# A transformer decoder layer on one core: the order in which each engine takes its tasks is replaced by another

## The reference

```python
x = x + attn(layernorm(x), Wq, Wk, Wv, Wo)            # 16 heads of 16, causal, alibi bias
x = x + xattn(layernorm(x), ctx, ctx, Wq, Wk, Wv, Wo) # 16 heads of 16, 120 keys
x = x + tanh(layernorm(x) @ weight @ aux_weight1 @ aux_weight2 + bias)
```

## Time and profile before

| | us |
|---|---|
| median of 3 runs | 2784.67 |
| lowest and highest of them | 2781.45, 2797.6 |
| profiled execution, time | 2791.88 |
| profiled execution, span from first to last instruction | 2790.1 |
| PE busy in the span | 2495.2 |
| DVE busy | 1714.9 |
| ACT busy | 1403.3 |
| POOL busy | 714.5 |

### The profile page before, as it was taken

How to read it: one execution, slowest core, us unless ns; L and a number is a source line. 1 busy time by engine, 2 the same in 40 slices (tenths; PEclk the granted TensorE clock), 3 DMA queues, 4 the chain that set the end, 5 groups by cost and what they waited for, 6 DMA issues and landing times.

```text
span 2790.1 us, 70718 instructions
## 1 busy us (share of the span) xinstructions
PE 2495.2 (89%) x23737; PEld 2048.2 (73%) x23864; DVE 1714.9 (61%) x3714; ACT 1403.3 (50%) x3067; POOL 714.5 (26%) x1359
## 2 busy tenths in 40 slices
...
GB/s 74 63 89 90 88 88 96 84 90 93 82 85 96 91 83 96 84 87 96 90 83 93 92 87 87 96 89 85 96 88 81 93 95 85 92 87 87 90 76 21
DMA packets 162889, 240.65 MB, mean 86 GB/s; under 512 B 21790, under 2 KB 86030, under 8 KB 159766
## 3 DMA queue, kind: packets, MB, share of 16 engines
...
...
## 4 chain that ended last, share of the span: by engine, by line
PE 57%; DMA 24%; DVE 6%; SPq 4%; issue 4%; ACT 4%; ACTq 1%; POOL 0%; DVEq 0%; POOLq 0%
DMA q_stack<-q_nat 12%; PE ps_misc L474 10%; DMA ctx_in<-in_ctx 9%; PE ps_misc L488 9%; PE ps_max L540 4%; SPq L394 4%; PE ps_score L585 3%; PE ps_score L572 3%; PE ps_max L553 3%; PE ps_attend L600 3%; PE ps_max L530 3%; PE ps_score L574 3%; PE ps_score L576 3%; PE ps_misc L630 2%; PE ps_max L536 2%
## 5 line engine op out<-in xcount | busy, mean ns | idle before, releaser
L901 DVE TENSOR_REDUCE neg_max_s<-ps_max 128x2 f32<-128x512 f32 (+1 forms) x768 | 483.1, 682 | 111.3 <-PE ps_max L530 73.0
L750 ACT ACTIVATE probs<-ps_score 128x384 f32<-128x384 f32 x1024 | 470.0, 492 | 141.3 <-PE ps_score L576 135.4
L757 ACT ACTIVATE xprobs<-ps_score 120x512 f32<-120x512 f32 x512 | 295.5, 599 | 244.4 <-PE ps_score L585 237.1
L1018 POOL TENSOR_SCALAR ve_LN<-mv_LN 128x2 f32<-128x2 f32 x192 | 36.8, 191 | 1342.7 <-DVE mv_LN L923 1342.7
L574 PE MATMUL ps_score<-q_stack,k_stack 97*128 97x256 f32 x1024 | 378.1, 369 | 0.0
L909 DVE TENSOR_REDUCE neg_max_x<-ps_max 128x4 f32<-128x480 f32 x512 | 314.2, 651 | 70.3 <-PE ps_max L553 70.3
L572 PE MATMUL ps_score<-mask_k,ident_b 128*128 128x256 bf16 x1024 | 290.9, 284 | 22.6 <-DMA q_stack<-neg_max_t_s 15.0
L576 PE MATMUL ps_score<-q_stack,k_stack 97*128 97x256 f32 x1024 | 291.1, 284 | 0.0
L1044 POOL TENSOR_TENSOR res<-res,chain_n 128x512 f32<-128x512 f32 x64 | 82.4, 1288 | 605.2 <-ACT chain_n L795 605.2
L585 PE MATMUL ps_score<-xq_stack,xk_stack 97*120 97x256 f32 x1024 | 227.2, 314 | 3.5 <-DMA xq_stack<-neg_max_t_x 2.8
L574 PEld LDWEIGHTS ps_score<-q_stack,k_stack 97*128 97x128 f32 x1024 | 206.6, 202 | 1.5
...
## 6 DMA issues: line engine op xcount, KB each, us to landing
k_stack<-k_nat SPq DMA_DIRECT2D x192, 256.0 KB, 6.9
q_stack<-q_nat SPq DMA_DIRECT2D x192, 256.0 KB, 7.2
xq_stack<-q_nat SPq DMA_DIRECT2D x192, 256.0 KB, 6.0
...
x_in<-in_x SPq DMA_DIRECT2D x64, 256.0 KB, 3.2
...
out_y<-res SPq DMA_DIRECT2D x64, 256.0 KB, 2.2
...
```

Source lines behind the costliest of these rows:

```text
L750: act.activation(probs[:, h % 8, :], bank_of("SCORE", i, b, h)[:, P:4 * P], ACT.Exp)\
L757: act.activation(xprobs[0:C, at:at + 2, :], blocks(bank_of("XSCORE", i, b, u))[0:C], ACT.Exp).then_inc(sem("xprobs_ready"), 1)
L901: dve.tensor_reduce(o, ins, AX.X, ALU.max, negate=True).then_inc(sem("max_taken"), 1)
```

## The change

All five tables are replaced. No instruction is added or taken away, no duration or size is changed; only the order on each engine, and with it the bank that each task gets, and the last step is one earlier (`END_STEP`), since the new tables need one step fewer to drain. Two lines of the tables and the constant, as the diff has them (each table is replaced as a whole, and its rows are better read in the order below):

```diff
 ORDER = {
     "SP": (
-        ("STORE", -3, 0), ("XMAX_STACK", -2, 0), ("LOAD_X", 1, 0), ("XK_STACK", -1, 0),
...
+        ("LOAD_X", 1, 0), ("XK_STACK", -1, 0), ("MAX_STACK", 0, 0), ("XQ_STACK", -1, 0),
+        ("LOAD_CTX", 0, 0), ("K_STACK", 1, 0), ("Q_STACK", 1, 0), ("STORE", -2, 0),
+        ("XMAX_STACK", -1, 0), ("XK_SAVE", 0, 0),
...
-FIRST_STEP, LOOP_FROM, LOOP_TO, END_STEP = -2, 6, 62, NSEQ + 3
+FIRST_STEP, LOOP_FROM, LOOP_TO, END_STEP = -2, 6, 62, NSEQ + 2
```

More of the change, by code:

```diff
@@ L68 @@
[L68 to L79, removed]
@@ L82 @@
+        ("LN2_T", 0, 0), ("XATTEND", -1, 1), ("MAX_T", 1, 0), ("XSCORE", -1, 6), ("XSCORE", -1, 7),
+        ("XQ", 0, 0), ("XATTEND", -1, 2), ("XATTEND", -1, 3), ("SCORE", 1, 0), ("SCORE", 1, 1),
+        ("XHEADS_OUT", -1, 0), ("XHEADS_OUT", -1, 1), ("SCORE", 1, 2), ("SCORE", 1, 3),
+        ("LN1_T", 2, 0), ("SCORE", 1, 4), ("SCORE", 1, 5), ("XOUT_T", -1, 0), ("ATTEND", 1, 0),
+        ("K", 2, 0), ("SCORE", 1, 6), ("SCORE", 1, 7),
     ),
     "ACT": (
-        ("SCORE", -1, 11), ("ATTEND", -1, 1), ("SCORE", -1, 12), ("SCORE", -1, 13),
@@ L85 @@
-        ("LN3_T", -3, 0), ("SCORE", -1, 14), ("SCORE", -1, 15), ("FFN", -3, 0), ("ATTEND", -1, 3),
-        ("V", 0, 0), ("XMAX_T", -2, 0), ("OUT_T", -1, 0), ("XSCORE", -2, 0), ("XSCORE", -2, 1),
-        ("XV", -1, 0), ("XSCORE", -2, 2), ("XSCORE", -2, 3), ("XSCORE", -2, 4), ("XSCORE", -2, 5),
-        ("XATTEND", -2, 1), ("XSCORE", -2, 6), ("XSCORE", -2, 7), ("LN2_T", -1, 0), ("MAX_T", 0, 0),
-        ("XATTEND", -2, 3), ("XQ", -1, 0), ("SCORE", 0, 0), ("SCORE", 0, 1), ("SCORE", 0, 2),
-        ("SCORE", 0, 3), ("LN1_T", 1, 0), ("SCORE", 0, 4), ("XOUT_T", -2, 0), ("K", 1, 0),
@@ L93 @@
+        ("LN3_T", -2, 0), ("SCORE", 0, 13), ("SCORE", 0, 14), ("CTX_T", 0, 0), ("SCORE", 0, 15),
+        ("FFN", -2, 0), ("ATTEND", 0, 3), ("XV", 0, 0), ("XMAX_T", -1, 0), ("OUT_T", 0, 0),
+        ("XK", 0, 0), ("XSCORE", -1, 0), ("XSCORE", -1, 1), ("V", 1, 0), ("XSCORE", -1, 2),
+        ("XSCORE", -1, 3), ("XSCORE", -1, 4), ("XSCORE", -1, 5), ("LN2_T", 0, 0), ("MAX_T", 1, 0),
+        ("XATTEND", -1, 1), ("XSCORE", -1, 6), ("XSCORE", -1, 7),
     ),
     "DVE": (
-        ("XMAX", -2, 2), ("XMAX", -2, 3), ("LN3_T", -3, 0), ("FFN", -3, 0), ("XMAX", -2, 4),
```

39 lines of the change are left out of this document (23 added, 16 removed).

## The result

The changed kernel takes 2816.3 us (median of 5 runs, 2798.73 to 2824.74) against 2790.8 of the kernel before on the same chip (5 runs). The ratio is 1.0088, with a 95% interval of 1.0054 to 1.0123: within 1%, as forecast, and on the slow side of it. Its profiled execution took 2798.73 us, the fastest of its five.

The account below looks back on a forecast made before the run. PE, 89% busy, was taken as the bound, with k and q transfers in turn setting when MAX starts. Cycle 81.0 plus 1.8 for the clock, 82.8 against 82.7, adds 3 us: 2795 profiled, 2788 median; range 2725 to 2856.

Parts of the forecast that it names:

- the sum at full clock: Four PE stretches added per step: 40.8 us even (with context work), 40.2 odd, a cycle of 81.0 us.
- MAX to OUT_PROJ: PE, first MAX to first OUT_PROJ matmul: 4.1 us even, 3.6 odd, the odd with 1.1 us standing for OUT_T.
- SCORE 0 to K: PE, first SCORE matmul to K's last: 6.45 us in both steps, bounds 6.3 and 6.8.
- The context wait: PE's 2.9 us wait for the context load in the even step: covered by work moved ahead, gone.
- K to MAX: PE, K's last matmul to first MAX: bound by k and q transfers in turn, 18.0 us even, 17.9 odd.
- OUT_PROJ to SCORE 0: PE, first OUT_PROJ to first SCORE matmul: grows by 1.1 us to 12.25 in both steps, bounds 0.2 and 1.5.
- DVE alone makes XQ late: Between OUT_PROJ and XQ: DVE's eight maxima instead of six delay LN2_T, so XQ starts at 1165.25 instead of 1164.99.
- the score stretch takes V for nothing: Faster rival, OUT_PROJ to SCORE 0: V fits into gaps, stretch grows 0.2 instead of 1.1 us; 2735 us, chance 0.27.
- XK_SAVE and XK_STACK: XK's save moved behind XMAX_STACK, its stack load ahead of MAX_STACK: cost nothing, cover 1.3 us.
- I leave the cost at 1.8: Slow PE clock behind waits: costs 1.8 us per cycle as before, bounds 0 and 5.0, making the cycle 82.8.
- The sign that was named: PE's granted clock over 1000 to 2500 us: 0.96 to 0.98; leaving that would show the forecast wrong.
- the clock falls behind both waits in every cycle: Slower rival, both waits before MAX: clock costs 4 us per cycle instead of 1.8; 2856 us, chance 0.27.

Follow-up runs that it names:

- experiment 1: The changed kernel with 246 skipped waits (123 instructions) ahead of PE's loop, moving its code; 2766.94 us, 0.9917 of the kernel before.
- Experiment 7: The changed kernel with the third of K's three transfers cut from 16 rows to one, so scores lack one product; 2630.49 us, one run.
- 8: The changed kernel with V alone put back ahead of XMAX 7 on PE and XV on ACT; 2744.69 us, 0.9841 of the kernel before.
- experiment 9: The changed kernel with V alone back in its old place and 123 instructions of skipped waits ahead of the loop; 2718.28 us, 0.9747 of before.
- experiment 10: The changed kernel with 123 skipped instructions and DVE's maxima 4 and 5 back ahead of OUT_PROJ's residual; 2770.08 us, 0.9928 of before.
- 11: The changed kernel with 123 skipped instructions and both V and DVE's maxima 4 and 5 back in their old places; 2709.82 us, 0.9718 of before.
- experiment 2: The kernel before with 266 skipped waits (133 instructions) ahead of PE's loop, moving its code; 2785.97 us, 0.9992 of the kernel before.

## Why the prediction was right or wrong

**The total** was 2788 and is 2816.3, within the range, and "within 1%" came true, with a gain and a loss behind it that nearly cancel. Without the stops the changed kernel is at 2767 (experiment 1), so the forecast was 21 us too high for what it reasoned about; the stops, about which it said nothing, add 49. That the sum of the two still lies in the range is luck. Of the 0.9 us by which the forecast cycle of 82.8 is above that of experiment 1 (81.94), the clock has 0.4 and the sum at full clock 0.4 to 0.5: three of its terms, MAX to OUT_PROJ in both steps and SCORE 0 to K, were each some 0.13 too high.

**The context wait** is gone, as forecast: no row of L507 for ctx_in is left.

**K to MAX** was called the sentence on which it all rests, 17.9 us in both steps. It is 18.2 in the even step and 18.1 in the odd one, with waits of 2.0 and 2.7 where 2.2 and 2.7 were given; 157.5 us in 64 waits where some 150 in 62 were. Experiment 7 shows the cause and 8 shows the other side, that 1.5 us of work put in there cost nothing.

**MAX to OUT_PROJ**: 3.96 for 4.1 in the even step. In the odd step a wait for DVE's chain_t comes as said, 0.7 us long behind the slow clock and 0.58 at full clock (experiment 9), where 1.1 was worked out. At full clock the stretch is 3.7 from the first weight load on (experiment 9), which by the cut of the forecast is 3.5 for 3.6.

**OUT_PROJ to SCORE 0** came to 12.2 as forecast. The steps inside it hold in part. The 1.1 us for XATTEND 2 and 3 behind XQ are there, measured at 0.8. The start of XQ, forecast 0.26 later, is: 9.64 us behind OUT_PROJ (1153.33 to 1162.97) instead of 9.34. The DVE row shows the eight maxima back to back, with a release of LN2_T at their end:

```profile
1155.06 0.69 DVE L955 TENSOR_TENSOR res<-ps_misc,x_in 128x512 f32<-128x512 f32 x1 [1.18 <-PE ps_misc L487]
...
1157.22 4.88 DVE L900 TENSOR_REDUCE neg_max_s<-ps_max 128x2 f32<-128x512 f32 x8 [0.28 <-issue]
1162.13 0.69 DVE L874 TENSOR_TENSOR chain_t<-ps_misc,chain_t 128x512 fp32r<-128x512 f32 x1
```

But that DVE alone makes XQ late is wrong. The way from OUT_PROJ to XQ, even / odd, is 9.3 / 9.3 us before and 9.6 / 9.6 after; it is 10.1 / 9.6 with DVE's order put back (experiment 10), 9.4 / 9.6 with V put back (9) and 9.4 / 9.3 with both (11). In the odd step either of the two is enough to make XQ late, and in the even step V is what does it. And the rival "the score stretch takes V for nothing" had half of the truth: V is nearly free there (0.3 us per cycle in experiment 9), but the stretch grows by 1 us all the same, for another reason, so its 2735 did not come.

**SCORE 0 to K**: 6.32 for 6.45. **XK_SAVE and XK_STACK** cost nothing, as forecast.

**The clock is the term that was mis-sized.** "I leave the cost at 1.8": it is 1.4 us in the cycle above, and 1.4 in the mean cycle of experiment 1 (81.94 less the 80.5 that its stretches add up to at full clock). The step failed in carrying over the 1.8 of before instead of asking behind which wait it falls and what work then runs slowly. Before, it fell behind each context wait of 2.9 in the thick of Q, SCORE and XK, and behind 6 of 24 waits of 2.0 (500 to 2500 us). After, it falls behind 18 of 24 odd waits, in front of MAX, and part of the slow work lies in the wait for chain_t; behind the even wait of 2.0 it does not fall in any of 19. The sign that was named, 0.96 to 0.98 from 1000 to 2500 us, came: 0.97 in the changed kernel and 0.98 in experiment 1. The rival "the clock falls behind both waits in every cycle" (2856) did not occur.

**Between the two shifted kernels**, 2 and 1, the mean cycle goes from 82.39 to 81.94, 12 us over the 27 cycles of the loop. The mean cycle of before itself differs between executions, 82.4 to 82.7 in three of them. Outside the loop, up to its first branch and from its last on, there are 563 us before (experiment 2) and 556 after (1). The forecast gave the drain nothing; 7 us lie there, and no run separates the shorter drain from the cycles that run outside the loop.

**Unforeseen** were two things. The wait for xq_stack before XMAX, 24.1 us in 54 pieces of 0.4, lies in the stretch K to MAX, which the transfers set anyway, and so costs nothing. The stops of PE at the loop's branch cost 31 us in the profiled execution, and 49 by the medians of the changed kernel and experiment 1.
